# A recurrent kernel on TensorE: the interleaved gate blocks go into one loop of four steps, with both operands in fixed buffers and 104 columns a block

## The reference

```python
x = x + _L0_cond_ref(x, cond_2048[:, None, :], ...)      # attention, 16 heads, with an output product
x = x + _L1_cond_ref(cond_2048, x, W_ih, W_hh, b_ih, b_hh)
x = x + _L2_cond_ref(x, cond_2048[:, None, :])           # causal convolution, 4 taps
x = x + _L3_cond_ref(x, cond_2048[:, None, :], b)        # the same, and a bias
```

```python
def cell(h, x):
    gi = x @ W_ih + b_ih
    gh = h @ W_hh + b_hh
    i_r, i_z, i_n = jnp.split(gi, 3, axis=-1)
    h_r, h_z, h_n = jnp.split(gh, 3, axis=-1)
    r = sigmoid(i_r + h_r); z = sigmoid(i_z + h_z)
    n = tanh(i_n + r * h_n)
    h_new = (1.0 - z) * n + z * h
```

## Time and profile before

| | before |
|---|---|
| median of 3 runs | 2255.23 us (2254.5 to 2259.69) |
| the profiled execution | 2253.05 us |
| its span, first to last instruction | 2251.1 us |
| start of the first step on TensorE | 621.7 us |
| start of the last step (the 512th) on TensorE | 2237.2 us |

### The profile page before, as it was taken

How to read it: one execution, slowest core, us unless ns; L and a number is a source line. 1 busy time by engine, 2 the same in 40 slices (tenths; PEclk the granted TensorE clock), 3 DMA queues, 4 the chain that set the end, 5 groups by cost and what they waited for, 6 DMA issues and landing times.

```text
span 2251.1 us, 183848 instructions
## 1 busy us (share of the span) xinstructions
PE 2137.5 (95%) x75456; PEld 1602.7 (71%) x75456; DVE 1396.2 (62%) x5052; ACT 1179.6 (52%) x5992; POOL 1136.2 (50%) x3895
## 2 busy tenths in 40 slices
PE   6899999999999999999999999999999999999997
PEld 1222222222399999989999988899999888888886
DVE  1434434444266776777677766777777777777775
ACT  2344444443255555555555555555555565555654
POOL 1142432333145555565555555655555666666665
PEclk8899999999999999999999999999999999999999
DMA  6000000001122221101222110022211000000000
GB/s 243 1 1 1 1 1 1 1 20 57 44 54 59 56 55 45 33 7 37 74 54 58 46 47 5 19 74 58 56 51 46 12 7 24 5 7 5 5 7 19
DMA packets 123332, 78.69 MB, mean 35 GB/s; under 512 B 18496, under 2 KB 119104, under 8 KB 122432
## 3 DMA queue, kind: packets, MB, share of 16 engines
q1 hardware_dynamic: 123056, 74.65, 11.9%
q10 hardware_dynamic: 144, 2.10, 0.2%
HBM read 26.37 MB, written 12.58 MB: 17 GB/s over the span
## 4 chain that ended last, share of the span: by engine, by line
PE 65%; DVE 6%; issue 2%; ACT 0%; POOL 0%; POOLq 0%; DVEq 0%
PE ps L1101 59%; PE ps L1128 5%; DVE arena L942 4%; DVE arena L959 1%; ACT ps L1034 0%; PE ps L1135 0%; POOL arena L1176 0%; ACT arena L1059 0%; DVE arena L992 0%; POOL arena L1180 0%; ACT arena L1065 0%; ACT arena L1070 0%; POOL arena L1182 0%; DVE seq L972 0%; DVE arena L980 0%
## 5 line engine op out<-in xcount | busy, mean ns | idle before, releaser
L1101 PE MATMUL ps<-whh,arena 128*4 128x128 f32 (+1 forms) x65536 | 1458.8, 246 | 56.3 <-DVE arena L959 43.0
L1101 PEld LDWEIGHTS ps<-whh,arena 128*4 128x4 f32 x65536 | 1335.3, 87 | 175.3 <-DVE arena L959 114.4
L1059 ACT ACTIVATE arena<-arena 128x8 f32<-128x8 f32 x1024 | 215.8, 211 | 685.5 <-DVE arena L942 677.4
L942 DVE STREAM_TRANSPOSE arena<-ps 128x128 f32<-128x128 f32 x1024 | 435.6, 425 | 207.4 <-PE ps L1101 203.9
L1176 POOL TENSOR_TENSOR arena<-tap,seq 128x32 f32<-128x32 f32 x1024 | 231.5, 258 | 288.6 <-DVE seq L972 288.6
L381 DVE TENSOR_REDUCE top<-ps 128x2 f32<-128x1024 f32 x128 | 150.7, 1219 | 258.2 <-PE ps L620 258.2
L959 DVE TENSOR_TENSOR_SCAN arena<-arena 128x24 f32<-128x24 f32 x1024 | 214.5, 209 | 145.0 <-ACT arena L1070 145.0
L1034 ACT ACTIVATE ps<-arena 128x128 f32<-128x128 f32 x1026 | 269.6, 263 | 0.3 <-PE ps L1135 0.3
L948 DVE STREAM_TRANSPOSE arena<-ps 128x64 f32<-128x64 f32 x1024 | 255.4, 249 | 19.2 <-PE ps L1101 9.9
L1176 POOL TENSOR_TENSOR arena<-tap,arena 128x32 f32<-128x32 f32 x1024 | 231.5, 257 | 66.8 <-POOL arena L1186 66.8
L523 PE MATMUL ps<-arena 128*32 128x512 f32 x2048 | 247.7, 604 | 11.5 <-POOL arena L214 11.5
(11 more groups left out here) (91 smaller groups left out, 1373.5 us busy)
## 6 DMA issues: line engine op xcount, KB each, us to landing
arena<-arena SPq DMA_DIRECT2D x384, 64.0 KB, 1.9
arena<-seq SPq DMA_DIRECT2D x192, 64.0 KB, 2.0
arena<-gi_d SPq DMA_DIRECT2D x256, 32.0 KB
gi_d<-arena SPq DMA_DIRECT2D x96, 64.0 KB, 1.6
seq<-in_x SPq DMA_DIRECT2D x4, 1024.0 KB, 17.3
whh<-in_w_hh SPq DMA_DIRECT2D x1, 3072.0 KB, 20.1
out<-seq SPq DMA_DIRECT2D x3, 1024.0 KB, 5.4
arena<-in_w_emb ACTq DMA_DIRECT2D x1, 2048.0 KB, 8.8
```

The costliest lines, as they stand in the source:

```text
L942: e.transpose(trn[:, h].rearrange("p q (i c s) -> p q c i s", c=2, s=2)[:, :, :, :, 0], bank[RN[h]][:, 0:P].rearrange("p (q c i) -> p q c ...
L1059: e.activation(r_d0[:, h].rearrange("p (i s) -> p i s", s=2)[:, :, 1], trn[:, h, 0, 0:2 * NH].rearrange("p (i s) -> p i s", s=2)[:, :, 0], ...
L1101: last = e.matmul(bank[dst[h]][32 * G:32 * G + B, 0:n], hv, wv[:, k, gates, G, 64 * h:64 * h + 64], start=False, stop=k2 == 1 and k == C - ...
```

## The change

All gate blocks are put into one list, `BLOCKS`, and one scheme serves them all.

* A block has 104 moving columns (`BW`) in place of 128. The 1024 columns of rz are covered by 10 blocks (the last one overlaps the one before it), the 384 tokens of n by 4 starts (the last one overlaps too). That gives 3 x 4 x 10 = 120 blocks of rz and 4 x 16 = 64 blocks of n: 184 blocks in 368 steps, two steps a block, from step 0 without a gap. Steps 368 to 511 have no blocks.
* The stationary operand is no longer read in place but copied by DMA into a new buffer `fixed`, again only where it differs from that of the block before. Chunks are brought in pairs: one DMA for two chunks (128 x 2 x 104), and one semaphore (`s_pair`) for each pair.
* With both operands in fixed buffers, TensorE's code is the same for each block. It is one loop of 92 passes with four steps and two blocks in its body, and then a loop of the 144 other steps, with two steps in its body.
* VectorE's code for the 368 steps is written out without a loop, with constants in place of registers. The blocks' own take is unchanged but for the width.

```diff
+        BW = 104
+        RZ_AT = [min(BW * j, 2 * D - BW) for j in range(-(-2 * D // BW))]
+        N_AT = [P + min(BW * j, T - P - BW) for j in range(-(-(T - P) // BW))]
+        BLOCKS = []
+        for i in range(TB - 1):
+            BLOCKS += [("rz", i + 1, b, first) for b in range(B) for first in RZ_AT]
+            for first in (N_AT[0:2], N_AT[2:3], N_AT[3:4])[i]:
+                BLOCKS += [("n", first, c, b) for c in range(C) for b in range(B)]
...
-        moving = tile([P, C, P])
+        fixed = tile([P, C, P])
+        moving = tile([P, C, BW])
...
-                    e.dma_start(moving[:, k, :], src).then_inc(s_moving[k], 16)
...
+                    if held == held_before:
+                        e.sem_inc(s_pair[v], 16)
+                    else:
+                        e.dma_start(fixed[:, ks, :], weights).then_inc(s_pair[v], 16)
+                    e.dma_start(moving[:, ks, :], src).then_inc(s_pair[v], 16)
...
+                for step in range(2, T, 2):
+                    q = step // 2 - 1
+                    if q < NBLOCKS:
+                        if q + 1 < NBLOCKS:
+                            for v in range(2):
+                                e.wait_ge(st["s_part"], 2 * q + v + 1)
+                                bring_pair(q + 1, v)
+                        keep(q)
...
+                    if step % P == 16 and step > P:
+                        store(e, *stores[step // P - 1])
...
+                for q in range(NBLOCKS):
+                    for v in range(2):
+                        step(2 * q + v, v)
+                    take(q)
+                with e.Fori(NBLOCKS, T // 2) as it:
+                    for v in range(2):
+                        step(it * 2 + v, v)
...
-                    for k in chunks:
-                        e.wait_ge(s_moving[k], e.snap(q * 16 + 16))
+                    e.wait_ge(s_pair[v], e.snap(q * 32 + 32))
+                    for k in (2 * v, 2 * v + 1):
                         for g in range(NG):
-                            last = e.matmul(bank[FB][32 * g:32 * g + 32, 0:P], stationary(k, g), moving[:, k, :],
+                            rows = slice(32 * g, 32 * g + 32)
+                            last = e.matmul(bank[FB][rows, 0:BW], fixed[:, k, rows], moving[:, k, :],
                                             start=k == 0, stop=k == C - 1)
...
+                with e.Fori(0, NBLOCKS // 2) as it:
+                    for w in range(2):
+                        q = e.snap(it * 2 + w)
                         for v in range(2):
-                            step(it * 2 + (first + v), v)
+                            step(q * 2 + v, v)
+                            part(v, q)
+                with e.Fori(NBLOCKS, T // 2) as it:
+                    for v in range(2):
+                        step(it * 2 + v, v)
```

136 lines of the change are left out of this document (44 added, 92 removed).

## The result

| | before | after |
|---|---|---|
| median of the runs compared | 2254.86 us (2252.0 to 2259.69) | 2216.82 us (2214.76 to 2218.45) |
| the profiled execution | 2253.05 us | 2214.76 us |
| its span | 2251.1 us | 2212.8 us |
| start of the first step on TensorE | 621.72 us | 617.84 us |
| start of the last step | 2237.23 us | 2199.31 us |

The ratio of the medians is 0.983 with a 95% interval of 0.9808 to 0.9844: the changed kernel is 38 us faster. The forecast was 2214 us, 2.8 us less. Of the 38.3 us of span, 34.0 lie in the steps and 3.9 before them, in a part whose code is the same; in the kernels of the experiments, which have the same first part, the first step started at 618.7 to 621.6 us, so I don't count these 3.9 us to the change.

The account below looks back on a forecast made before the run. Bare steps were taken as bound by the chain TensorE, VectorE, ScalarE, VectorE, alternate block steps also by the loop's end. 836.3 + 297.2 + 5.2 + 3 + 432.6 = 1574.3 us against 1615.5 gave 2214 us, range 2200 to 2242.

Parts of the forecast that it names:

- the long and the short step: TensorE steps with blocks before the change: 3.27 us for the second of a two-step body, 3.03 for the first.
- the long step is not the loop's end: Rival: the 0.24 us belong to each second part, so block steps keep 3.15 us; 25.7 us more, 2240; 6 in 100.
- Steps without a loop's end: TensorE's 276 block steps that do not end a body: 3.03 us each, 836.3 us in all.
- Steps with a loop's end: TensorE's 92 block steps that end a body: 3.23 us each (between 3.19 and 3.27), 297.2 us in all.
- 104 columns bring nothing: Claim for the 276 block steps not ending a body: narrower parts save no time, since the chain decides.
- VectorE, 3 us, from 0 to 15: Allowance in block steps for VectorE's takes of n and for scans of line 954 starting beside GpSimd's line 1180.
- VectorE's straight code: Rival: 28 instruction packets for VectorE's written-out code each stop it about 1.1 us; 31 us, 2245; 4 in 100.
- Loop entries: First passes of TensorE's loops: 24 entries with blocks go; what remains costs 5.2 us, from 2 to 10.
- SyncE: Operand loads on the queues: hidden, 3.6 us against 6.1, except 1.4 us late behind the 1 MB store in two places.
- the rival of late operands: Each change of `fixed` is late by 1 to 2 us; 28 to 56 us come back, 2242 to 2270; 5 in 100.
- Bare steps: Steps without blocks on TensorE: 143 at 3.025 us, 432.6 us in all.
- The body that does not fit: Rival: TensorE's 4.5-block body is refetched in each of 92 passes; 120 to 460 us more, 2334 to 2670; 7 in 100.

## Why the prediction was right, and where not

**What bounded the kernel** was read rightly. The 0.24 us between the long and the short step were the loop's end: it is in the fourth step of a body of four, in every second step of a body of two, and in the kernel without GpSimd it is 3.22 - 3.02 = 0.20 us with no scan held up. What two bodies save by becoming one is a little less, 0.16. The rival "the long step is not the loop's end" (2240 us) is out: three steps of four lost it.

**Steps without a loop's end**, 276 x 3.03 = 836.3 us. Three kinds measured 3.12, 3.07 and 3.01. Without the meeting they are 3.03, 3.02 and 3.01: I was 0.03 us a pass too high there, 3 us in all.

**Steps with a loop's end**, 92 x 3.23: measured 3.22, inside the range that 104 columns left open.

**"104 columns bring nothing" in the other steps** is true for this change (3.12, 3.07, 3.01 with either width) and false as a reason. "The chain decides" held because a scan made the chain late; where no scan does, the wide block costs 0.06 us in two more of the four steps.

**VectorE, 3 us, from 0 to 15: the term that was mis-sized.** The mechanism was the right one, a scan of line 954 beside GpSimd's line 1180, and I had both rows. What failed is the step "The long steps set that meeting; now most steps are short". The long steps did not set it: with VectorE's straight code alone and TensorE's steps as before, the scans of n were held up in 195 of 288 block steps instead of 59. It was this part of the change, which I had expected to bring or cost nothing but stops for its own fetches, that moved GpSimd's addition ahead of the scan. And I took the meeting for an accident of a few passes, but steps of fixed lengths in a loop repeat the phase, so it came in most of them: 12.42 - 12.28 = 0.14 us, x 91 = 12.7 us. The takes of n, the other half of the term, show nothing.

**Loop entries, 5.2 us.** The first pass costs 16.08 - 12.42 = 3.7 us over a quiet one and the entry into the bare loop 0.2, together 3.9. Of the 3.7, 1.6 lie in the very first step, most of it at a granted clock of 0.50, which was slow before too (3.91 us); the three steps behind it lost 2.0, where I had put 3 or more for the blocks. For the kernel before, the 24 first bodies of its loops can be summed:

```profile
sum 176.40, PE 160.61 PEld 147.00 DVE 111.80 ACT 89.50 POOL 91.70; mean PE 6.69 PEld 6.12 DVE 4.66 ACT 3.73 POOL 3.82
```

That is 176.40 - 24 x 6.30 = 25.2 us of the 30.9 over quiet bodies, about 1 us each as the forecast had it; the 120 other bodies hold the rest, 5.7. In one loop with a body of two (1162.1 us for 184 bodies of 6.30 us) 2.9 are left, 1.4 of them in its first body. So 23 entries were 23.8 us, and the other bodies were 4.2 us longer in all, the sum of narrower blocks and more meetings, which no run takes apart. Against that, the 80 steps that get blocks now take 252.0 us (40 bodies at 6.30) where they took 244.9 without (97.34 + 99.11, and 16 at 3.025): 23.8 + 4.2 - 7.1 = 20.9 us, which is also the difference of the first 368 steps (1183.0 against 1162.1). With the 13.3 us of the loop's ends that is 34.2 us, against 34.0 in all the steps. So of what was gained nearly 24 us are loop entries and 13 loop's ends.

**SyncE.** A pair of 104 KB lands in 2.1 us, as worked out, `fixed` in 2.1 to 2.2, and no change of `fixed` makes a part wait; the rival of late operands is out. Behind the 1 MB store I had 1.4 us late in two places and left it out of the sum. It is 1.1 and 0.9 us, 2.1 in all with the step behind each.

**VectorE's straight code** (2245 us) is out as a rival: its fetches stop nothing, by an edit of its own. That it moved GpSimd's addition is told above.

**Bare steps**: 432.6 forecast, 432.7 measured.

**The body that does not fit** was the rival on the slow side, and the sign of it was right: q8 packets in each pass. Its price was not: the kernel with eight steps brings 500 packets more, near the 414 blocks of 92 x 4.5, and is 673 us slower than the changed one, where I had 120 to 460. I had only the stops inside a pass; a stop of 4.5 to 5.0 us at the jump back and a step at half the clock come on top, and no row of before could show either.

**The sum.** Against the 1574.3 us: the pass 12.42 for 12.32 x 91 = +9.1, the allowed 3 used up, the first pass -1.0, the stores +2.1, bare steps with their entry -0.4, and 0.4 unnamed: +7.2 us, which is 1581.5. The part before the recurrence gave back 3.9 us and the end 0.4, so the span missed by only 2.9. The forecast was nearer than its terms.

## What to carry to other kernels

A loop's end on the engine that is last costs most of its price in each pass, and the first pass of a loop body about 1 us for 2.25 blocks of instructions and 3 us for 4.5: fewer, longer bodies pay until a body no longer stays with the engine. Beyond that edge the loss is far larger than the gain (6.75 blocks cost 279 us over 4.5 at the same width), so look in the profile for instruction packets after the first pass. Code that is made shorter on an engine with time to spare can still shift a third one into the chain's way, which the total may hide. In a loop of fixed step lengths an operation on an engine off the critical path can meet the same instruction of the chain in pass after pass; when a step kind comes out 0.1 us long, look at what runs beside its scans, and move that by phase. A width that brings nothing today was only hidden behind another wait: try it again when that wait is gone.

## What the runs showed of the hardware

* A VectorE scan of 16 elements that starts while a GpSimd addition runs ends 0.04 us after the addition (0.28 and 0.34 us long), and one that starts 0.07 us before it takes 0.19.
* TensorE kept a body of 1152 instruction records (4.5 blocks of 16 KB) through the 91 passes behind the first without a packet; with 1728 two and seven packets came in turn, and every second pass ran without a stop inside; with 2304 about eleven came in each. The jump back into a body that is no longer held stopped TensorE for 4.5 to 5.1 us; behind one such stop the granted clock was 0.51, and 128 loads took 4.97 us for 2.67.
* GpSimd's addition, which starts when VectorE's addition to `seq` lets its products go, came 0.07 us sooner when VectorE's register instructions and loop's ends were gone (2.27 us into the step for 2.34).
* A memset of 8 columns ahead of GpSimd's four products was hidden, and the addition behind them started 0.05 us sooner.
